# State space stage of a twelve-stage decoder: the causal convolution moved from VectorE to TensorE, the activations split off and done 1024 wide

## The chip, the core and the metric

One core of a Trainium2 chip runs the whole program. The time is the device time of one execution in microseconds, before as the median of three runs. In the profile PE is TensorE (PEld its weight loads), DVE is VectorE, ACT is ScalarE, POOL is GpSimd.

## What is computed

A decoder of four layers on 64 sequences of 64 tokens and 128 channels. The change lies in the seventh of its twelve stages, a Mamba-like state space block in float32:

```python
xr = x @ w_in + b_in                      # x normalised, 128 -> 512
xc, res = jnp.split(xr, 2, axis=-1)       # 256 channels each
u = jax.nn.silu(_causal_conv(xc, w_conv, b_conv))   # 4 taps along time
A = -jnp.exp(A_log)
dt, B, C = jnp.split(u @ w_x, [DTR, DTR + N], axis=-1)   # 64, 16, 16
delta = jax.nn.softplus(dt @ w_dt)
deltaA = jnp.exp(delta[..., None] * A)
deltaBu = delta[..., None] * B[:, :, None, :] * u[..., None]
h = a * h + bu                            # scan over the 64 steps, for each of N = 16 states
y = jnp.einsum('bldn,bln->bld', hs, C) + u * D
return y * jax.nn.silu(res) @ w_out
```

and `_causal_conv` is the bias plus the sum over k of `xp[:, k:k + l, :] * w_conv[k]`, with xp padded by three zero steps.

## The kernel before

The tokens are worked in NG = 8 groups g of 512 (eight sequences). Channels lie on the partitions, in two chunks c of 128, so a tile is 128x512. Within a group the 16 states k are the innermost loop. The program calls one (g, k) an iteration m = 16g + k; here it is called a slot.

Each engine has its own program, written out by hand, and semaphores join them. In slot m (line numbers are those of the profile):

- VectorE does `scan(m, 0)`, `contribute(m-1, 1)`, `scan(m, 1)`, `contribute(m, 0)` (L2131 the scan, L2139 its product with the row of C), then whatever is hung on this k: two convolution taps for the next group at k = 0 to 3 (`tap`, L2105 and L2108), `skipped` at the head of k = 1 (L2144), `residual` of the group before (L2149) and `ln.stats` at k = 4, `parts` (L2115 to L2122, splits B and C into three bf16 parts) at k = 6, `scale` (L658) at k = 9.
- ScalarE does `decay(m+1, 0)` (L2013, the exponential that the next scan reads), `copy_b(m+2)` (L2002), `decay(m+1, 1)`, then: `silus` at k = 4 (L1963, L1966), `copy_dt` at 5 (L1972), `high_part` at 6 (L1979), `step_size` at 7 and 8 (L1986, L1987), `softplus` at 9 (L1992 Exp, L1995 Ln), `copy_ln` and `channels` at 12 to 14 (L1947, L1955). Silu, Exp and Ln each want another table; ACT_TABLE_LOAD is put in where the function changes.
- TensorE does `accumulate(m-1, 0)` (L1898, hc times identity into a bank), `b_row(m+2)` and `c_row(m+1)` (L1876, which spread a row of B or C over the partitions), `accumulate(m-1, 1)`, then: `output` of the group before at k = 3 (L163), m2 and m3 at 4 (L1852), dt and bc at 5 and 6 (L1859), d0 and d1 at 7 and 8 (L1867), `turn` (L1845), m0, m1 at 12 to 14.
- GpSimd does the two products of `inputs(m+1)` (L2065), then `gated` at k = 2 (L2079), the norm's `rstd` at 5, `step_size` at 10 and 11 (L2070, L2073).

All the side steps of TensorE share one bank, `misc` (bank 7). `ssm_order` gives each its number; `take` waits until the step before it has been copied out (`misc_cp`), `have` waits until this one has been written (`misc_mm`). c_row is double buffered, b_row is not.

## Time and profile before

| | |
|---|---|
| median of 3 runs | 4207.73 us (4207.13 to 4212.16) |
| the profiled execution | 4205.07 us, its span 4203.3 us |
| busy shares | PE 88%, DVE 53%, ACT 37%, POOL 27% |
| the state space stage | from 2072.99 (first memset) to 2764.20 + 0.69 us (last residual) |
| granted TensorE clock, whole program | 0.912 |

Shares over the whole span say little here, since this change touches one stage of some 690 us; the stage's own windows and its timeline count.

### The profile page before, as it was taken

The numbers are of one execution on the slowest core, as the hardware profiler recorded it, in microseconds if no ns is written. First come the engines' busy times: TensorE is split into PE (matmuls) and PEld (weight loads), VectorE is DVE, ScalarE is ACT, GpSimd is POOL, SyncE is SP. The second block draws the span as 40 slices with busy tenths as digits, with TensorE's granted clock in tenths as the row PEclk, the third lists the DMA queues.
The fourth block names the chain that finished last, engine by engine and source line by source line (L and its number), as shares of the span: only waits on it lengthen the run. The fifth ranks groups of instructions, "written<-read, shape, count | busy, mean of one in ns | idle before, by whom it ended". The sixth has DMA issues, their size and how long they took to land. (4 is left out here: it accounts for less than half of the span.)

```text
span 4203.3 us, 78999 instructions
## 1 busy us (share of the span) xinstructions
PE 3692.2 (88%) x32473; PEld 2458.5 (58%) x32473; DVE 2212.7 (53%) x4913; ACT 1561.4 (37%) x2468; POOL 1145.7 (27%) x1165
## 2 busy tenths in 40 slices
PE   4988889998999988999867777786778999999998
PEld 2655567776777655666422222244448888767776
DVE  2645522222766655555478888855556556422222
ACT  3422233332111034222254555543225565434343
POOL 2534400001222154000056566643451011010111
PEclk8978889999999989999978878897789999999999
DMA  4000000000000010000100000000000000000000
GB/s 144 2 1 1 1 1 1 1 1 34 3 3 2 6 39 7 1 1 1 43 0 1 0 1 0 1 1 1 1 1 12 5 7 5 2 3 3 6 6 6
DMA packets 20276, 37.11 MB, mean 9 GB/s; under 512 B 848, under 2 KB 17488, under 8 KB 19280
## 3 DMA queue, kind: packets, MB, share of 16 engines
q1 hardware_dynamic: 19920, 32.07, 2.2%
q8 instruction: 260, 4.26, 0.4%
q14 instruction: 96, 0.79, 0.1%
HBM read 29.97 MB, written 2.10 MB: 8 GB/s over the span
## 5 line engine op out<-in xcount | busy, mean ns | idle before, releaser
L163 PEld LDWEIGHTS ps<-L_ffn_w,arena 128*128 128x128 f32 x5248 | 615.5, 193 | 58.3 <-issue 45.0
L649 POOL TENSOR_SCALAR arena<-arena 128x4 f32<-128x4 f32 x120 | 27.6, 230 | 2250.6 <-DVE arena L641 1913.7
L163 PE MATMUL ps<-L_ffn_w,arena 128*128 128x128 f32 x5248 | 627.1, 277 | 0.0
L751 PE MATMUL ps<-arena,L_ffn_w 128*128 128x512 f32 x1024 | 464.9, 597 | 0.0
L2065 POOL TENSOR_TENSOR arena<-arena 128x512 f32<-128x512 f32 x256 | 327.3, 1303 | 234.9 <-ACT arena L2002 234.3
L785 DVE SCALAR_TENSOR_TENSOR x_all<-ps,arena,x_all 128x128 f32<-128x128 f32 x512 | 144.2, 345 | 400.7 <-PE ps L163 400.7
L1898 PE MATMUL ps<-arena,const_w 128*128 128x512 f32 x512 | 325.1, 733 | 33.4 <-DVE arena L2144 20.7
L2131 DVE TENSOR_TENSOR_SCAN arena<-ps,arena 128x512 f32<-128x512 f32 x256 | 311.3, 1216 | 72.6 <-ACT ps L2013 56.1
L751 PEld LDWEIGHTS ps<-arena,L_ffn_w 128*128 128x128 f32 x1024 | 186.5, 192 | 186.7 <-issue 184.8
L163 PEld LDWEIGHTS ps<-L_attn_w,arena 128*128 128x128 f32 x1984 | 254.2, 197 | 61.5 <-issue 44.6
L163 PE MATMUL ps<-L_attn_w,arena 128*128 128x128 f32 x1984 | 283.7, 289 | 5.1 <-POOL arena L2079 2.7
L775 ACT ACTIVATE arena<-ps,L_ffn_w 128x512 f32<-128x512 f32 x256 | 174.5, 687 | 267.9 <-PE ps L751 267.8
L953 PE MATMUL ps<-arena,L_ffn_w 128*128 128x512 f32 x576 | 261.2, 596 | 0.8 <-ACT arena L986 0.8
L775 ACT ACTIVATE arena<-ps 128x512 f32<-128x512 f32 x256 | 152.1, 597 | 273.4 <-PE ps L751 273.2
L2013 ACT ACTIVATE ps<-arena,aneg 128x504 f32<-128x504 f32 x256 | 174.9, 683 | 200.9 <-DVE arena L2131 200.2
L785 DVE SCALAR_TENSOR_TENSOR arena<-ps,arena 128x128 f32<-128x128 f32 x256 | 72.1, 344 | 324.0 <-PE ps L163 324.0
L1876 PE MATMUL ps<-bcp,sel 96*128 96x512 bf16 x256 | 106.6, 451 | 112.3 <-DVE arena L2139 88.1
L1898 PEld LDWEIGHTS ps<-arena,const_w 128*128 128x128 f32 x512 | 108.5, 225 | 146.3 <-DVE arena L2139 77.8
L996 ACT ACTIVATE arena<-ps 128x512 f32<-128x512 f32 x144 | 86.0, 597 | 279.8 <-PE ps L953 231.7
L430 ACT ACTIVATE arena<-ps 128x1024 f32<-128x1024 f32 x96 | 98.4, 1025 | 235.1 <-PE ps L332 235.1
L1249 PE MATMUL ps<-arena,L_attn_w 128*128 128x512 f32 x384 | 183.8, 615 | 0.9 <-ACT arena L712 0.9
L1317 ACT ACTIVATE arena<-ps,L_attn_w 128x512 f32<-128x512 f32 x64 | 44.0, 687 | 347.5 <-PE ps L1249 347.5
(351 smaller groups left out, 6538.6 us busy)
## 6 DMA issues: line engine op xcount, KB each, us to landing
L_ffn_w<-L_ffn SPq DMA_DIRECT2D x1, 4312.0 KB, 14.1
L_ffn_w<-L_ffn SPq DMA_DIRECT2D x1, 4120.5 KB, 14.5
...
```

The costliest lines, as they stand in the source:

```text
L163: ins = pe.matmul(out, src[:, j * P:(j + 1) * P], w, start=(i == 0), stop=(bias is None and i == len(chunks) - 1))
L430: a.activation(pts(i), e.bank(0, 2), ACT.Copy).then_inc(s["pt_cp"], 1)
L751: pe.matmul(e.bank(f), up(x, f), xT(g), start=True, stop=True).then_inc(s["up_mm"], 1)
L775: a.activation(hidden(i)[:, f * GT:(f + 1) * GT], e.bank(f), func, bias=bias(x, f)).then_inc(s["act_done"], 1)
L785: ins = v.scalar_tensor_tensor(out=a, in0=e.bank(4 + i % 2)[:, j * D:(j + 1) * D], scalar=weight(j), in1=a, op0=ALU.mult, op1=ALU.add)
L953: pe.matmul(e.bank(2 * k + c), wt, src, start=True, stop=True).then_inc(s["gu_mm"], 1)
L1249: pe.matmul(e.bank(i), W(w)[:, col], xnT(g), start=True, stop=True).then_inc(s["qkg_mm"], 1)
L1876: return pe.matmul(out, e.sel[:, row:row + 1].broadcast_to([96, P]), bcp(g), start=True, stop=True)
L1898: pe.matmul(acc(c), e.ident, hc(m, c), start=(k == 0), stop=(k == N - 1)).then_inc(s["acc_mm"], 1)
L2013: a.activation(tiles(at(c), NB)[:, :, 1:S], tiles(delta(g, c), NB)[:, :, 1:S], ACT.Exp, scale=e.aneg[:, c * N + k:c * N + k + 1]).then_inc ...
L2065: q.tensor_tensor(bu(m, c), du(g, c), bs(m), ALU.mult).then_inc(s["bu_done"], 1)
L2131: v.tensor_tensor_scan(hs(m, c), at(c), bu(m, c), 0.0, ALU.mult, ALU.add).then_inc(s["hs_done"], 1)
```

## The change

The four taps become four matmuls that accumulate in the misc bank, each with a 128x128 diagonal matrix of tap weights as the stationary operand (`taps`, made once in the startup, in the free tiles pq and pk2) and a shifted view of xp as the moving one. ScalarE copies the result out with the bias (`raw`, Identity), also m2 and m3, and applies Silu later, in one place, to 1024 columns at a time; Exp and Ln of softplus, `step_size` and `gated` of GpSimd also become 1024 wide. `ssm_order` gets the steps cv0 and cv1, and the side steps move: output from k = 3 to 4, m2 and m3 to 5 and 6, silus from 4 to 6, dt and bc to 7 and 8, parts from 6 to 9, d0 and d1 to 10 and 11, softplus to 11, GpSimd's step_size to 12, ln.stats to 6, rstd to 7, scale to 11, turn, m0, m1 to 13 to 15.

```diff
--- before.py
+++ after.py
@@ -1791,9 +1791,11 @@
...
-    for step, g in [(x, 0) for x in "ln m0 m1 m2 m3 dt bc d0 d1".split()] + [(x, 1) for x in "ln m0 m1".split()]:
+    for step, g in [(x, 0) for x in "ln m0 m1 cv0 cv1 m2 m3 dt bc d0 d1".split()] + [(x, 1) for x in "ln m0 m1".split()]:
...
+        if g + 1 < NG:
+            use["cv0", g + 1], use["cv1", g + 1] = len(use), len(use) + 1
@@ -1810,20 +1812,21 @@
-        two = lambda t: lambda c: t[:, c * GT:(c + 1) * GT]
...
-        xp_all, tmp = room.take(2 * NB * (S + 3)), two(room.take(2 * GT))
+        xp_all, raw_u = room.take(2 * NB * (S + 3)), room.take(2 * GT)
+        taps = lambda c, i: (e.pq, e.pk2)[c][:, i * P:(i + 1) * P]
@@ -1850,6 +1853,18 @@
+            def convolve(c, g, which):
+                if which[0] == 0:
+                    take(("cv0", "cv1")[c], g)
+                    pe.wait_ge(s["misc_cp"], use[("m0", "m1")[c], g] + 1)
+                    if g == 0:
+                        pe.wait_ge(s["taps_done"], 1)
+                for i in which:
+                    ins = pe.matmul(tiles(misc, NB), taps(c, i), xp(c)[:, :, i:i + S],
+                                    start=(i == 0), stop=(i == 3))
+                if which[-1] == 3:
+                    ins.then_inc(s["misc_mm"], 1)
@@ -1898,8 +1913,12 @@
-            for step in ("m0", "m1", "m2", "m3"):
-                channels(step, 0)
+            channels("m0", 0)
+            channels("m1", 0)
+            for c in range(2):
+                convolve(c, 0, range(4))
+            channels("m2", 0)
+            channels("m3", 0)
@@ -1916,21 +1935,22 @@
-                if k == 3 and g >= 1:
+                if k == 4 and g >= 1:
...
                 if g + 1 < NG:
-                    if k == 4:
-                        channels("m2", g + 1)
-                        channels("m3", g + 1)
+                    if k < 4:
+                        convolve(k // 2, g + 1, ((0, 1), (2, 3))[k % 2])
                     if k in (5, 6):
-                        projected(("dt", "bc")[k - 5], g + 1)
+                        channels(("m2", "m3")[k - 5], g + 1)
                     if k in (7, 8):
-                        step_size(("d0", "d1")[k - 7], g + 1)
+                        projected(("dt", "bc")[k - 7], g + 1)
+                    if k in (10, 11):
+                        step_size(("d0", "d1")[k - 10], g + 1)
                 if g + 2 < NG:
-                    if k == 12:
+                    if k == 13:
...
-                    if k in (13, 14):
-                        channels(("m0", "m1")[k - 13], g + 2)
+                    if k in (14, 15):
+                        channels(("m0", "m1")[k - 14], g + 2)
@@ -1951,19 +1971,29 @@
...
-                    a.wait_ge(s["conv_done"], 2 * (g - 1) + c + 1)
+                    a.wait_ge(s["misc_mm"], use[("cv0", "cv1")[c], g - 1] + 1)
...
+            def raw(step, g):
+                c = int(step[-1]) % 2
+                have(step, g)
+                if step[0] == "c":
+                    if g >= 1:
+                        a.wait_ge(s["u_done"], 2 * g)
+                    out, bias = raw_u[:, c * GT:(c + 1) * GT], W("b_conv")[:, c:c + 1]
+                else:
+                    if g >= 2:
+                        a.wait_ge(s["yr_done"], 2 * (g - 1))
+                    out, bias = res(g, c), W("b_in")[:, 2 + c:3 + c]
+                a.activation(out, misc, ACT.Identity, bias=bias).then_inc(s["misc_cp"], 1)
             def silus(g):
-                for c in range(2):
-                    a.wait_ge(s["conv_done"], 2 * g + c + 1)
-                    if g >= 2 and c == 0:
-                        a.wait_ge(s["misc_mm"], use["y", g - 2] + 1)
-                    a.activation(u(g, c), tmp(c), ACT.Silu, bias=W("b_conv")[:, c:c + 1]).then_inc(s["u_done"], 1)
-                for c in range(2):
-                    have(("m2", "m3")[c], g)
-                    a.activation(res(g, c), misc, ACT.Silu, bias=W("b_in")[:, 2 + c:3 + c]).then_inc(s["misc_cp"], 1)
+                a.wait_ge(s["misc_cp"], use["m3", g] + 1)
+                if g >= 2:
+                    a.wait_ge(s["misc_mm"], use["y", g - 2] + 1)
+                a.activation(u_b(g), raw_u, ACT.Silu).then_inc(s["u_done"], 2)
+                a.activation(res_b(g), res_b(g), ACT.Silu).then_inc(s["res_done"], 1)
@@ -1988,11 +2018,9 @@
...
-                for c in range(2):
-                    a.activation(du(g, c), du(g, c), ACT.Exp, scale=-1.0).then_inc(s["sp_own"], 1)
-                a.wait_ge(s["sp_own"], 2 * (g + 1))
-                for c in range(2):
-                    a.activation(du(g, c), du(g, c), ACT.Ln, bias=1.0).then_inc(s["sp_done"], 1)
+                a.activation(du_b(g), du_b(g), ACT.Exp, scale=-1.0).then_inc(s["sp_own"], 1)
+                a.wait_ge(s["sp_own"], g + 1)
+                a.activation(du_b(g), du_b(g), ACT.Ln, bias=1.0).then_inc(s["sp_done"], 1)
@@ -2009,13 +2037,15 @@
                     if k == 0:
-                        a.wait_ge(s["dl_done"], 2 * g + c + 1)
+                        a.wait_ge(s["dl_done"], g + 1)
...
+            for step in ("cv0", "cv1", "m2", "m3"):
+                raw(step, 0)
@@ -2035,21 +2065,25 @@
                 if g + 1 < NG:
-                    if k == 4:
+                    if k in (1, 3):
+                        raw(("cv0", "cv1")[k // 2], g + 1)
+                    if k in (5, 6):
+                        raw(("m2", "m3")[k - 5], g + 1)
+                    if k == 6:
...
-                    if k == 5:
+                    if k == 7:
...
-                    if k == 6:
+                    if k == 8:
...
-                    if k in (7, 8):
-                        step_size(k - 7, g + 1)
-                    if k == 9:
+                    if k in (10, 11):
+                        step_size(k - 10, g + 1)
+                    if k == 11:
...
                 if g + 2 < NG:
-                    if k == 12:
+                    if k == 13:
...
-                    if k in (13, 14):
-                        channels(k - 13, g + 2)
+                    if k in (14, 15):
+                        channels(k - 14, g + 2)
@@ -2059,55 +2093,41 @@
                         if k == 0:
-                            q.wait_ge(s["du_done"], 2 * g + c + 1)
+                            q.wait_ge(s["du_done"], g + 1)
...
-            def step_size(c, g):
-                q.wait_ge(s["relu_done"], 2 * g + c + 1)
-                q.wait_ge(s["sp_done"], 2 * g + c + 1)
-                q.tensor_tensor(delta(g, c), delta(g, c), du(g, c), ALU.add).then_inc(s["dl_done"], 1)
-                q.wait_ge(s["dl_done"], 2 * g + c + 1)
-                q.wait_ge(s["u_done"], 2 * g + c + 1)
-                q.tensor_tensor(du(g, c), delta(g, c), u(g, c), ALU.mult).then_inc(s["du_done"], 1)
+            def step_size(g):
+                q.wait_ge(s["relu_done"], 2 * (g + 1))
+                q.wait_ge(s["sp_done"], g + 1)
+                q.tensor_tensor(delta_b(g), delta_b(g), du_b(g), ALU.add).then_inc(s["dl_done"], 1)
+                q.wait_ge(s["dl_done"], g + 1)
+                q.wait_ge(s["u_done"], 2 * (g + 1))
+                q.tensor_tensor(du_b(g), delta_b(g), u_b(g), ALU.mult).then_inc(s["du_done"], 1)
...
             def gated(g):
-                q.wait_ge(s["misc_cp"], use["m3", g] + 1)
-                for c in range(2):
-                    q.wait_ge(s["yo_done"], 2 * g + c + 1)
-                    q.tensor_tensor(u(g, c), u(g, c), res(g, c), ALU.mult).then_inc(s["yr_done"], 1)
+                q.wait_ge(s["res_done"], g + 1)
+                q.wait_ge(s["yo_done"], 2 * (g + 1))
+                q.tensor_tensor(u_b(g), u_b(g), res_b(g), ALU.mult).then_inc(s["yr_done"], 2)
...
-            step_size(0, 0)
-            step_size(1, 0)
+            step_size(0)
...
-                if k in (10, 11) and g + 1 < NG:
-                    step_size(k - 10, g + 1)
-                if k == 5 and g + 2 < NG:
+                if k == 12 and g + 1 < NG:
+                    step_size(g + 1)
+                if k == 7 and g + 2 < NG:
...
         @block.vector
         def _(v):
-            def tap(g, c, i):
-                t, w, x = tiles(tmp(c), NB), W("w_conv")[:, c * 4 + i:c * 4 + i + 1], xp(c)[:, :, i:i + S]
-                if i == 0:
-                    v.wait_ge(s["misc_cp"], use[("m0", "m1")[c], g] + 1)
-                    if g >= 1:
-                        v.wait_ge(s["u_done"], 2 * (g - 1) + c + 1)
-                    v.tensor_scalar(t, x, w, None, ALU.mult).then_inc(s["conv_own"], 1)
-                else:
-                    v.wait_ge(s["conv_own"], 3 * (2 * g + c) + i)
-                    v.scalar_tensor_tensor(out=t, in0=x, scalar=w, in1=t, op0=ALU.mult, op1=ALU.add
-                                           ).then_inc(s[("conv_own", "conv_done")[i == 3]], 1)
@@ -2161,7 +2181,8 @@
-                    tap(0, c, i)
+                    ins = v.tensor_scalar(taps(c, i), e.ident, W("w_conv")[:, 4 * c + i:4 * c + i + 1], None, ALU.mult)
+            ins.then_inc(s["taps_done"], 1)
@@ -2172,18 +2193,14 @@
-                if g + 1 < NG:
-                    if k < 4:
-                        for i in ((0, 1), (2, 3))[k % 2]:
-                            tap(g + 1, k // 2, i)
-                    if k == 6:
-                        parts(g + 1)
+                if k == 9 and g + 1 < NG:
+                    parts(g + 1)
...
                 if g + 2 < NG:
-                    if k == 4:
+                    if k == 6:
...
-                    if k == 9:
+                    if k == 11:
```

VectorE from k = 1 to k = 4 of a group, before. L2144 is skipped, L2149 residual, L635 and L641 ln.stats:

```order
L2144 SCALAR_TENSOR_TENSOR arena<-arena,L2_attn_w,ps 128x512 x2
L2131 SCALAR_TENSOR_TENSOR arena<-ps,arena 128x512
L2139 TENSOR_TENSOR arena<-arena,ps 128x512
...
L2108 SCALAR_TENSOR_TENSOR arena<-arena,L2_attn_w 128x512 x2
L2131 SCALAR_TENSOR_TENSOR arena<-ps,arena 128x512
...
L2149 TENSOR_TENSOR x_all<-ps,x_all 128x512
L635 BN_STATS arena<-x_all 128x6 x4
```

The same place with the change (L2164 skipped, L2151 scan, L2159 contribute, L2169 residual):

```order
L2164 SCALAR_TENSOR_TENSOR arena<-arena,L2_attn_w,ps 128x512 x2
L2151 SCALAR_TENSOR_TENSOR arena<-ps,arena 128x512
L2159 TENSOR_TENSOR arena<-arena,ps 128x512
...
L2169 TENSOR_TENSOR x_all<-ps,x_all 128x512
L2151 SCALAR_TENSOR_TENSOR arena<-ps,arena 128x512
```

The taps are gone from between the scans, ln.stats has left k = 4, and the residual is still the last of k = 4.

TensorE around the output of the group before (L163), before; a 128x512 x2 of L1876 is one slot's b and c row:

```order
L1876 MATMUL ps<-bcp,sel 128x512 x2
L1898 MATMUL ps<-arena,const_w 128x512
L163 MATMUL ps<-L2_attn_w,arena 128x128 x8
L1898 MATMUL ps<-arena,const_w 128x512
L1876 MATMUL ps<-bcp,sel 128x512 x2
L1898 MATMUL ps<-arena,const_w 128x512
L1852 MATMUL ps<-arena,L2_attn_w 128x512 x2
```

With the change (L1913 accumulate, L1891 rows, L1864 convolution, L1855 m2):

```order
L1864 MATMUL ps<-arena,pk2 128x512 x2
L1913 MATMUL ps<-arena,const_w 128x512
L1891 MATMUL ps<-bcp,sel 128x512 x2
L1913 MATMUL ps<-arena,const_w 128x512
L163 MATMUL ps<-L2_attn_w,arena 128x128 x8
L1913 MATMUL ps<-arena,const_w 128x512
L1891 MATMUL ps<-bcp,sel 128x512 x2
L1913 MATMUL ps<-arena,const_w 128x512
L1855 MATMUL ps<-arena,L2_attn_w 128x512
```

Two taps now stand at the end of each of the slots 0 to 3, the output at the end of slot 4, and m2 in slot 5. (A float32 matmul of this list is two MATMUL rows in the trace.)

ScalarE around the activations, before:

```order
L2013 ACTIVATE ps<-arena,aneg 128x8x63
L1963 ACT_TABLE_LOAD
L1963 ACTIVATE arena<-arena,L2_attn_w 128x512 x2
L1966 ACTIVATE arena<-ps,L2_attn_w 128x512 x2
L2013 ACT_TABLE_LOAD
L2013 ACTIVATE ps<-arena,aneg 128x8x63
```

With the change (L1989 raw, L1995 and L1996 the two Silus, L2041 decay):

```order
L1989 ACTIVATE arena<-ps,L2_attn_w 128x512
L1995 ACT_TABLE_LOAD
L1995 ACTIVATE arena<-arena 128x1024
L1996 ACTIVATE arena<-arena 128x1024
L2041 ACT_TABLE_LOAD
L2041 ACTIVATE ps<-arena,aneg 128x8x63
```

Between the two table loads nothing waits for TensorE any more; the last raw copy stands right ahead of them.

## Rows read from the trace of the kernel before

**Rows 1.** Groups by line and one line's own view (min/median/max ns), stage's window.

```profile
L2131 DVE TENSOR_TENSOR_SCAN arena<-ps,arena 128x512 f32<-128x512 f32 x256 | 311.3, 1216 | 72.6 <-ACT ps L2013 56.1 <-POOL arena L2065 14.5
...
L2108 DVE SCALAR_TENSOR_TENSOR arena<-arena,L_attn_w x48: 750/1631/1648, 2082.7 to 2639.5; 128x512 f32<-128x512 f32 x48
```

**Rows 2.** Windows: us, busy of PE, PEld, DVE, ACT, POOL, granted clock.

```profile
2356.00:2436.00 80.00, 58.17 (x125) 20.85 (x124) 66.71 (x88) 42.09 (x66) 45.52 (x37) 0.83 0.00 1
...
2676.00:2756.00 80.00, 60.49 (x146) 20.90 (x145) 76.90 (x92) 43.93 (x69) 59.34 (x48) 0.94 0.00 1
```

**Rows 3.** Timeline of VectorE, fourth group: start, us, then the instruction.

```profile
2364.50 1.22 DVE L2131 TENSOR_TENSOR_SCAN arena<-ps,arena 128x512 f32<-128x512 f32 x1
...
2370.17 1.39 DVE L2144 SCALAR_TENSOR_TENSOR arena<-arena,L_attn_w,ps 128x512 f32<-128x512 f32 x2
2371.49 1.21 DVE L2131 TENSOR_TENSOR_SCAN arena<-ps,arena 128x512 f32<-128x512 f32 x1
...
2389.03 1.21 DVE L2131 TENSOR_TENSOR_SCAN arena<-ps,arena 128x512 f32<-128x512 f32 x1
...
2392.45 0.68 DVE L2149 TENSOR_TENSOR x_all<-ps,x_all 128x512 f32<-128x512 f32 x1
```

**Rows 4.** The same timeline: VectorE's waits in one group (in brackets).

```profile
2400.77 1.22 DVE L2131 TENSOR_TENSOR_SCAN arena<-ps,arena 128x512 f32<-128x512 f32 x1 [3.05 <-ACT ps L2013]
...
2408.97 0.69 DVE L2115 TENSOR_TENSOR arena<-ps,bcp 32x512 f32<-32x512 f32 x1 [4.69 <-ACT bcp L1979]
...
2419.84 1.22 DVE L2131 TENSOR_TENSOR_SCAN arena<-ps,arena 128x512 f32<-128x512 f32 x1 [1.03 <-ACT ps L2013]
...
2425.46 1.22 DVE L2131 TENSOR_TENSOR_SCAN arena<-ps,arena 128x512 f32<-128x512 f32 x1 [0.84 <-ACT ps L2013]
...
2432.07 1.22 DVE L2131 TENSOR_TENSOR_SCAN arena<-ps,arena 128x512 f32<-128x512 f32 x1 [3.10 <-ACT ps L2013]
```

**Rows 5.** Waits over the stage: total us, times, longest.

```profile
DVE arena L2131 <- ACT ps L2013: 56.1, 29, 4.2
...
DVE arena L2115 <- ACT bcp L1979: 36.8, 8, 9.8
```

**Rows 6.** Timeline of ScalarE around silus.

```profile
2392.69 1.28 ACT L1963 ACT_TABLE_LOAD   x1
...
2400.05 0.68 ACT L2013 ACTIVATE ps<-arena,aneg 128x504 f32<-128x504 f32 x1
```

**Rows 7.** Groups by line, whole span: a 1024-wide activation from SBUF.

```profile
L424 ACT ACTIVATE arena<-arena 128x1024 f32<-128x1024 f32 x96 | 101.3, 1055 | 98.7 <-DVE arena L542 98.4
```

**Rows 8.** Timeline of TensorE: at either clock.

```profile
2387.11 2.60 PE L163 MATMUL ps<-L_attn_w,arena 128*128 128x128 f32 x16
...
2413.82 0.59 PE L1876 MATMUL ps<-bcp,sel 96*128 96x512 bf16 x1 [4.23 <-DVE arena L2139]
...
2424.62 0.60 PE L1876 MATMUL ps<-bcp,sel 96*128 96x512 bf16 x2
2425.05 1.88 PE L1898 MATMUL ps<-arena,const_w 128*128 128x512 f32 x4
...
2434.39 3.62 PE L1898 MATMUL ps<-arena,const_w 128*128 128x512 f32 x4
```

**Rows 9.** Timeline of GpSimd.

```profile
2385.61 2.95 POOL L2065 TENSOR_TENSOR arena<-arena 128x512 f32<-128x512 f32 x2 [2.99 <-ACT arena L2002]
...
2401.33 2.49 POOL L2065 TENSOR_TENSOR arena<-arena 128x512 f32<-128x512 f32 x2 [5.57 <-ACT arena L2002]
...
2429.66 1.26 POOL L2070 TENSOR_TENSOR arena<-arena 128x512 f32<-128x512 f32 x1 [1.14 <-ACT arena L1995]
```

**Rows 10.** Timeline of the startup.

```profile
2085.04 2.07 PE L1852 MATMUL ps<-arena,L_attn_w 128*128 128x512 f32 x2 [0.78 <-ACT arena L1955]
...
2092.10 3.31 PE L1859 MATMUL ps<-arena,L_attn_w 128*64 128x512 f32 x4 [0.78 <-ACT arena L1966]
...
2115.92 2.45 DVE L2131 TENSOR_TENSOR_SCAN arena<-ps,arena 128x512 f32<-128x512 f32 x2 [14.51 <-POOL arena L2065]
```

2 lines of the change are left out of this document (1 added, 1 removed).

## Prediction

> **What bounds the kernel now.** The change touches one stage, so the first view is the windows of the state space stage, not the shares of the page. In a middle window of 80 us VectorE is busy 66.7 us, TensorE 58.2, ScalarE 42.1, GpSimd 45.5; in the window that is mostly the last group, where no side work is left, VectorE is busy 76.9 of 80 [rows 2]. Then the timeline of VectorE, to see what fills a slot: two scans and two products. From 2389.03 to 2392.45 nothing else stands, so a bare slot is 3.42 us [rows 3]. Sixteen of them are 54.7 us. What a group takes above that is side work on VectorE and waits of VectorE. So the reader should look for (a) what else VectorE executes, and (b) which waits end last there. The waits of one group stand in [rows 4]; their totals over the stage are 56.1 us for decays that come late and 36.8 us for the high part of B and C, eight times, the longest of them (9.8) in the startup [rows 5]. A scan waiting for ScalarE does not mean that ScalarE is full; it is half idle. It means that one block of its program (table load, Silu, table load) is longer than the lead it has over the scans.
>
> **What the change removes.** *The taps.* From the scan at 2364.50 (k = 0) to the residual at 2392.45 (end of k = 4) are 27.95 us. Five bare slots are 17.1 and skipped is 1.32 (2371.49 less 2370.17), so the taps cost 9.5 us a group [rows 3]. Seven groups have them inside the loop: 66.5 us. In the first of these the scans of k = 1 wait for a decay that ScalarE issues late after its copies for group 1; the two taps of slot 0 lie under that wait and are worth nothing: less 2.2.
>
> That price contains contention: one tap with two operands takes from 0.75 to 1.65 us, its median 1.63 [rows 1], and the GpSimd pair beside taps takes 2.95 instead of 2.49 us [rows 9]. The GPSIMD Engine Reference of the Trainium skill (section 1, Specifications) says that GpSimd's SBUF interfaces are shared with VectorE and contend with VectorE instructions that have two SBUF inputs. That agrees with these rows. Priced without the contention, as VectorE work alone, eight taps at the minimum of 0.75 would be 6.0 us a group, 42 in all; priced by slots they are 66.5. I take the slots, since they hold what really stood on the path.
>
> *The wait of parts.* bc, high_part and parts were in one slot, so VectorE stood still for TensorE and ScalarE: 36.8 less the 9.8 of the startup is 27.0 us [rows 5]. With bc in slot 8 and parts in 9 there is a whole slot between: gain 27.0. The five instructions of parts stay.
>
> **What it moves.** *silus.* Before, ScalarE's block lasts from the table load at 2392.69 to the end of the next decay at 2400.73, 8.0 us, because m3 waits for the copy of m2 in its middle; the scan waits 3.05 [rows 4, 6]. Now two loads of 1.28 [rows 6], two Silus of 1.06 [rows 7] and the decay of 0.68, 5.4 us, behind the raw copy of m3. Counted from the start of slot 6: decay(7,1) ends at 3.7, TensorE has m3 at 3.9, raw ends 4.65, the decay for slot 8 ends at 10.0. VectorE wants it after two slots and ln.stats (1.2), at 8.05. Wait 2.0, in the last such group (no ln.stats) 3.2. Before, 3.05 in five groups, 3.65 in the first and 4.22 in the last of them (the longest of [rows 5]), 23 us; after, six by 2.0 and 3.2, 15. Gain 8.
>
> *d0, d1, softplus.* Before, in one group, 1.03 + 0.84 + 3.10 = 5.0 us [rows 4], over the seven about 32 (56.1 less the silus waits and the 0.9 after the start [rows 5]). Now softplus follows d1 in the same slot. From the relu of d1: two copies 1.1, Exp 1.06, load 1.28, Ln 1.06, load 1.28, decay 0.68, 6.5 us. When d1 is ready depends on TensorE's clock. Parts leave TensorE idle for some 3.7 us ahead of slot 10, and behind such an idle time of 4.23 us it ran at half clock, four matmuls in 3.62 us against 1.88 [rows 8]. At half clock d0 costs 1.1 us of wait in slot 10 and d1 4.5 in slot 11, together 5.6; at full clock 2.5. I take the half clock, by the nearest row: 39 in seven groups against 32, a loss of 7; the bound at full clock is a gain of 15.
>
> *GpSimd's step_size.* Two operations of 1024, each twice 1.26 [rows 9], now start together after Ln. Let X be the end of the first decay after softplus. Ln ended at X - 1.97, the sum at X + 0.6, the product at X + 3.2, and only then comes inputs(14, 0), done at X + 4.5. Its scan wants it at X + 3.4: a new wait of 1.1 us, 7.5 in all. inputs is what is queued behind it on GpSimd, and the scan waits for that.
>
> *The output of the group before.* It moved to k = 4 on TensorE, the residual on VectorE stays at k = 4. Before, a slot lay between, and the residual waited for nothing. Now TensorE starts the output after accumulate(m-1, 1), about 3.0 us into the slot plus what it lags, and needs 2.6 us [rows 8]; VectorE asks at 3.4. The lag comes from the convolution: a slot of 0 to 3 needs four accumulate matmuls and four for two taps (1.7 us each at full clock, from 1.88 less the drain) and two rows (0.43), 3.85 us against 3.42 [rows 8]. With skipped as slack it ends some 1.2 us behind at k = 4. So the residual waits 2.2 without lag, 3.6 with it. I take 3.6 for six groups and 2.2 for the last (no convolution in it): 23.8 lost.
>
> *Convolution on TensorE.* Its lead over VectorE absorbs the 0.4 us a slot: b_row may come over 2 us late before a scan waits. raw at k = 1 and 3 must wait for it, which delays a decay by up to 0.3; bc at slot 8 by up to 0.4. I charge 0.7 a group, 5 in all; bounds 0 and, at half clock, the rival below. The strided moving operand has no row; nearest is the contiguous one, 0.43 a matmul.
>
> *Startup and tail.* The tap diagonals (eight 128x128 products) lie under m0 and m1 and cost nothing. Then in line: m2 started at 2085.04, once m1 was copied [rows 10]; the first convolution starts there in its place; 5.2 us partly at half clock, raw 0.8, 3.5, raw 0.8, two round trips of 1.8 for m2 and m3, the first Silu 1.1: dt at 2100 instead of 2092.10 [rows 10]. With the wider first step of GpSimd 8.5 us lost. gated at the end waits for both halves: 0.8.
>
> **Sum.** 66.5 - 2.2 + 27 + 8 - 7 - 7.5 - 23.8 - 5 - 8.5 - 0.8 = 46.7. The profiled execution took 4205.07 us; 46.7 less is 4158.4. The median is 2.7 above the profiled one, so 4161.
>
> **Rivals.** *More gain.* TensorE, with less idle time, stays at full clock in slots 10 and 11 (22 more), and the output lags less (8 more), perhaps raw and bc cost nothing (5): 4126 to 4145. For it: 0.94 granted where slots are bare, against 0.83 [rows 2]. Against: the idle time behind parts stays.
>
> *Slower: TensorE becomes the bound in the convolution slots.* At half clock such a slot is 3.62 for accumulates, 3.62 for taps, 0.9 for rows, less drains 7.7 us, against 3.42 [rows 8]. Four slots are 17.1 us over, less a lead of 2.4: 14.7 by seven groups is 103, so 4264. It decides from a bit over two of the four slots at half clock, since 46.7 / 7 = 6.7 us. For it: the clock in the stage is 0.83 [rows 2], and the end of softplus now comes two slots later, nearer to k = 0. Against: once packed, TensorE came back to full clock within two to three slots, and in these slots it has almost no gap. On this the page TensorE: Matmul & The Clock Gate of the Trainium skill (section Why this matters for your kernels) says that sustained matmul work brings the full clock; by that rule too the slots would run full, and the time would be the forecast's.
>
> *Longer tail of softplus.* One or two more scans wait for GpSimd's late inputs, or the residual waits out a cold output (3.5 instead of 2.6): 2 to 4 us a group more, 4175 to 4193.
>
> *It does little.* Waits take the place of the taps: every slot from 0 to 3 ends with ScalarE held in raw, 5 to 7 us a group: 4196 to 4216.
>
> **Chances.** Forecast (4145 to 4175) 0.50, more gain 0.20, longer tail 0.14, little 0.07, slower 0.09. The range runs from 4128 to 4193 and leaves out the tail of more gain, little and slower. A measurement of this kernel tells about 0.2% (8.4 us) from no change. Faster by more than that (below 4199) 0.85, within it 0.06, slower 0.09.
>
> **What would show it.** In the profile after: no gap between scans in slots 0 to 3 but skipped, and a slot of 3.4 us there; parts without a wait; the first scan after the Silus waiting 2 us; the scan after softplus waiting 4 to 5 us, and the next one 1 us for GpSimd; the residual waiting 2 to 4 us for TensorE in seven groups, the longest new wait; the first scan near 2124. The period of a middle group comes to some 75 us (54.7 bare, 7 of side work, 13 of these waits). The prediction is wrong if slots 0 to 3 take over 4.5 us, if the convolution matmuls show half clock in most groups, or if the residual finds its output ready.

## The result and the profile after

Four runs of the changed kernel have a median of 4164.57 us (4160.2 to 4165.26), four of the kernel before beside them 4208.27. The ratio is 0.9892, its 95% interval 0.9875 to 0.9909, so 43.7 us less. The forecast was 4161 with a range from 4128 to 4193. The profiled execution of after is the slowest of its four, 4165.26 us, against 4205.07 before: 39.8 less, and against this number the parts are held below. Of the experiments' executions two, 5188.81 us in experiment 5 and 4912.06 us in experiment 9, ran at a granted clock of 0.67 and 0.71 instead of some 0.91, and every median below is that of the others.

VectorE's waits after, engine, line, releaser, then total us, times, longest. They answer to [rows 5] (L2151 is the scan, L2135 the start of parts, L2169 the residual):

```profile
DVE arena L2151 <- ACT ps L2041: 72.7, 26, 7.7
DVE arena L2135 <- ACT bcp L2009: 27.3, 1, 27.3
DVE x_all L2169 <- PE ps L163: 24.6, 8, 6.2
```

The wait for the high part stands eight times in [rows 5] and once here, in the startup. In its place the residual waits for TensorE eight times, and the scans wait longer for ScalarE. So the waits have not become less; they have moved: summed over the loop (defined below) those of VectorE are 83 us before and 91 after. The 24.6 of the residual hold 6.2 of the stage's tail.

The timeline of VectorE after, in the startup and in the second group (columns as in [rows 3]):

```profile
2105.81 0.69 DVE L2135 TENSOR_TENSOR arena<-ps,bcp 32x512 f32<-32x512 f32 x1 [27.33 <-ACT bcp L2009]
...
2124.15 2.44 DVE L2151 TENSOR_TENSOR_SCAN arena<-ps,arena 128x512 f32<-128x512 f32 x2 [15.58 <-POOL arena L2099]
...
2203.95 1.40 DVE L2164 SCALAR_TENSOR_TENSOR arena<-arena,L_attn_w,ps 128x512 f32<-128x512 f32 x2
...
2221.89 0.69 DVE L2169 TENSOR_TENSOR x_all<-ps,x_all 128x512 f32<-128x512 f32 x1 [2.84 <-PE ps L163]
...
2236.07 1.22 DVE L2151 TENSOR_TENSOR_SCAN arena<-ps,arena 128x512 f32<-128x512 f32 x1 [2.05 <-ACT ps L2041]
...
2243.77 0.86 DVE L2137 CAST bcp<-arena 32x512 bf16<-32x512 f32 x1
2244.66 1.37 DVE L2138 CAST bcm<-arena 32x512 bf16<-32x512 f32 x1
...
2264.88 1.22 DVE L2151 TENSOR_TENSOR_SCAN arena<-ps,arena 128x512 f32<-128x512 f32 x1 [6.07 <-ACT ps L2041]
...
2269.08 1.22 DVE L2151 TENSOR_TENSOR_SCAN arena<-ps,arena 128x512 f32<-128x512 f32 x1 [0.69 <-ACT ps L2041]
...
2279.36 1.40 DVE L2164 SCALAR_TENSOR_TENSOR arena<-arena,L_attn_w,ps 128x512 f32<-128x512 f32 x2
```

From one skipped to the next are 2279.36 less 2203.95, 75.4 us, where the prediction had some 75. The reader sees the four waits in their order: the output late for the residual (2.84), the Silu block (2.05), the block of softplus (6.07), GpSimd behind it (0.69). Parts have no wait any more, but two of their five instructions, the casts L2137 and L2138, are longer than before.

TensorE in the same group: first a slot of the convolution (L1864), then the idle time behind parts and d0, d1 (L1882).

```profile
2212.17 1.88 PE L1864 MATMUL ps<-arena,pk 128*128 128x512 f32 x4
...
2216.04 1.88 PE L1864 MATMUL ps<-arena,pk 128*128 128x512 f32 x4
...
2249.28 0.38 PE L1891 MATMUL ps<-bcp,sel 96*128 96x512 bf16 x1 [4.77 <-DVE arena L2159]
2249.50 1.83 PE L1913 MATMUL ps<-arena,const_w 128*128 128x512 f32 x2
2251.26 2.07 PE L1882 MATMUL ps<-arena,L_attn_w 64*128 64x512 f32 x2
...
2257.15 1.12 PE L1882 MATMUL ps<-arena,L_attn_w 64*128 64x512 f32 x2
```

One slot of the convolution takes 3.87 us (2216.04 less 2212.17) at full clock, and in the view no row between the two has a wait. The shifted views that the taps read cost nothing extra: four such matmuls (L1864) take 1.88 us, like four with a contiguous operand (L1913). Behind 4.77 us of idle time d0 takes 2.07 us, at the lower clock of 1.2 GHz (called half clock here); d1 takes 1.12, at 2.4 GHz again (full clock). d0 takes 2.07 in all seven groups, d1 in two of them, the ones where the wait of softplus is 7.70. ScalarE and GpSimd in the block of softplus:

```profile
2258.31 0.60 ACT L2016 ACTIVATE arena<-ps 128x512 f32<-128x512 f32 x1 [1.33 <-PE ps L1882]
...
2262.87 1.28 ACT L2041 ACT_TABLE_LOAD   x1
2264.16 0.68 ACT L2041 ACTIVATE ps<-arena,aneg 128x504 f32<-128x504 f32 x1
```

```profile
2262.99 2.34 POOL L2104 TENSOR_TENSOR arena<-arena 128x1024 f32<-128x1024 f32 x1 [4.02 <-ACT arena L2023]
2265.41 2.35 POOL L2107 TENSOR_TENSOR arena<-arena 128x1024 f32<-128x1024 f32 x1
2267.72 7.42 POOL L2099 TENSOR_TENSOR arena<-arena 128x512 f32<-128x512 f32 x6
```

The first product for the next slot starts at 2267.72 and ends some 1.23 us later, at 2268.95; the scan starts at 2269.08. The row of that scan names ScalarE, but the decay it reads had ended before; it waited for GpSimd. Experiment 2 tests this reading.

**Where the 39.8 went.** The profiles are cut at three points: the stage's first memset, the first scan, the last skipped, the last residual. From memset to first scan are 42.93 us before and 53.34 after, 10.4 lost. From the first scan to the last skipped (here called the loop) are 641.07 and 592.53, 48.5 gained. The rest of the stage is 7.21 and 7.79. Together 37.6; the other 2.2 lie ahead of the stage, which the change doesn't touch. The loop is the number that the experiments below are compared by, since it leaves out what differs ahead of the stage and behind it from one execution to the next.

### The profile page after: what moved, and what is told of

Same layout as the page of the kernel before. It is cut to its first block and busy times, and to the rows that moved or that the text cites. A ratio compares the mean times of both kernels' runs of the same rounds, so it can differ in the third digit from the quotient of the medians.

```text
span 4163.5 us, 79189 instructions
## 1 busy us (share of the span) xinstructions
PE 3689.2 (89%) x32601; PEld 2467.4 (59%) x32601; DVE 2152.8 (52%) x4857; ACT 1574.9 (38%) x2468; POOL 1131.4 (27%) x1141
## 5 line engine op out<-in xcount | busy, mean ns | idle before, releaser
L163 PEld LDWEIGHTS ps<-L_ffn_w,arena 128*128 128x128 f32 x5248 | 615.4, 193 | 58.3 <-issue 45.0
L163 PE MATMUL ps<-L_ffn_w,arena 128*128 128x128 f32 x5248 | 627.0, 277 | 0.0
L2151 DVE TENSOR_TENSOR_SCAN arena<-ps,arena 128x512 f32<-128x512 f32 x256 | 312.2, 1219 | 90.0 <-ACT ps L2041 72.7
L1913 PE MATMUL ps<-arena,const_w 128*128 128x512 f32 x512 | 290.5, 656 | 7.5 <-DVE arena L2159 6.4
L163 PE MATMUL ps<-L_attn_w,arena 128*128 128x128 f32 x1984 | 277.9, 285 | 5.8 <-POOL arena L2112 3.4
L163 PEld LDWEIGHTS ps<-L_attn_w,arena 128*128 128x128 f32 x1984 | 247.5, 193 | 59.5 <-issue 42.6
L2041 ACT ACTIVATE ps<-arena,aneg 128x504 f32<-128x504 f32 x256 | 174.6, 682 | 134.5 <-DVE arena L2151 134.3
L1891 PE MATMUL ps<-bcp,sel 96*128 96x512 bf16 x256 | 96.8, 412 | 114.6 <-DVE arena L2159 81.7
L2159 DVE TENSOR_TENSOR arena<-arena,ps 128x512 f32<-128x512 f32 x256 | 170.0, 664 | 0.0
## 6 DMA issues: line engine op xcount, KB each, us to landing
L_attn_w<-L_attn SPq DMA_DIRECT2D x1, 3153.0 KB, 21.2
```

What stands on the lines that cost most here:

```text
L163: ins = pe.matmul(out, src[:, j * P:(j + 1) * P], w, start=(i == 0), stop=(bias is None and i == len(chunks) - 1))
L1913: pe.matmul(acc(c), e.ident, hc(m, c), start=(k == 0), stop=(k == N - 1)).then_inc(s["acc_mm"], 1)
L2041: a.activation(tiles(at(c), NB)[:, :, 1:S], tiles(delta(g, c), NB)[:, :, 1:S], ACT.Exp, scale=e.aneg[:, c * N + k:c * N + k + 1]).then_inc ...
L2151: v.tensor_tensor_scan(hs(m, c), at(c), bu(m, c), 0.0, ALU.mult, ALU.add).then_inc(s["hs_done"], 1)
L2159: v.tensor_tensor(hc(m, c), hs(m, c), cbank(m), ALU.mult).then_inc(s["hc_done"], 1)
```

## The experiments

### 1. The residual into slot 5

The residual is put behind the second scan of slot 5, so that the output has time.

```diff
                 scan(m, 1)
+                if k == 5 and g >= 1:
+                    residual(g - 1)
                 contribute(m, 0)
...
-                if k == 4 and g >= 1:
-                    residual(g - 1)
```

> The changed kernel, with the residual of the group before moved on VectorE from the end of slot 4 into slot 5, behind its second scan; TensorE's output stays in slot 4. Theory (the residual waits 2.83 us in six groups and 1.5 in the last because output and residual share a slot): the wait goes, 18 us less than the changed kernel, about 4146; no wait at the residual. Rival (the wait only moves: m2 in slot 5 needs the bank that the residual frees, so raw, the decay behind it and a scan come late): less than 6 us gained, 4159 to 4165, and a new wait of a scan for ScalarE in slot 6 or 7.

Median 4161.14 us (4156.76 to 4161.58), ratio 0.9887 (0.9872 to 0.9902), loop 585.04: 7.5 us gained of 18.5 that had been waited. The theory had the wait gone, which it is, but 18 us less; the time is the rival's, though not by its mechanism alone. The wait of the residual is gone, and others are longer. The waits of VectorE over the run and the timeline of TensorE in the second group:

```profile
DVE arena L2151 <- ACT ps L2041: 83.5, 31, 7.7
```

```profile
2248.05 0.59 PE L1891 MATMUL ps<-bcp,sel 96*128 96x512 bf16 x1 [4.76 <-DVE arena L2159]
...
2250.27 2.07 PE L1882 MATMUL ps<-arena,L_attn_w 64*128 64x512 f32 x2
...
2256.84 2.07 PE L1882 MATMUL ps<-arena,L_attn_w 64*128 64x512 f32 x2
```

The scans wait 10.8 us more for ScalarE. Now d1 too is at half clock and the wait of softplus is 7.70 in six groups: 7.5 us more over the seven. The one after the Silus is 2.61 instead of 2.05, 3.4 us more. So a wait may be worth less than its length: part of what is freed comes back at the next block, here most of it where d1 is at half clock.

### 2. GpSimd's sum and product in two slots

The sum stays in slot 12, the product goes to 13, and `inputs` of one slot comes between.

```diff
                 if k == 12 and g + 1 < NG:
-                    step_size(g + 1)
+                    step_sum(g + 1)
+                if k == 13 and g + 1 < NG:
+                    step_product(g + 1)
```

> The changed kernel, with GpSimd's sum in slot 12 and its product in slot 13 instead of both in 12. Theory (the scan of slot 14 waits for inputs(14, 0) behind 4.7 us of step_size; the profile puts 0.69 us of it down to ScalarE's decay, which had long ended): the second wait after softplus, 0.69 us in seven groups, goes, about 5 us less, 4160. Rival (it is the decay, as the profile names it): nothing changes, 4164 to 4165, the wait stays.

Median 4157.54 (4155.6 to 4158.93), ratio 0.9882 (0.9865 to 0.9898), loop 586.62. GpSimd:

```profile
2259.45 2.34 POOL L2104 TENSOR_TENSOR arena<-arena 128x1024 f32<-128x1024 f32 x1 [4.70 <-ACT arena L2023]
2261.90 2.49 POOL L2099 TENSOR_TENSOR arena<-arena 128x512 f32<-128x512 f32 x2
2264.35 2.35 POOL L2109 TENSOR_TENSOR arena<-arena 128x1024 f32<-128x1024 f32 x1
```

The seven waits of 0.69 are gone, all of them, though every one was put down to ScalarE. So they were GpSimd's.

### 3. The whole of softplus one slot later

```diff
-                    if k == 11:
+                    if k == 12:
                         softplus(g + 1)
...
-                if k == 12 and g + 1 < NG:
+                if k == 13 and g + 1 < NG:
                     step_size(g + 1)
```

> The changed kernel, with softplus in slot 12 and GpSimd's step_size in 13, each one slot later; d1 stays in slot 11. Theory (d1 comes late at half clock and softplus starts only when d1 has been copied, so the two delays add up; in the kernel before they cost 0.84 and 3.10 in two slots): the wait after softplus falls from 6.07 to about 3.1, a wait of up to 1.1 stands in slot 12 or 13, together 1.5 to 2 us less in seven groups, 4150 to 4154. Rival (it is the length of the block alone, 6.5 us from the relu on): the wait stays over 5, 4160 to 4167.

Median 4156.7 (4144.21 to 4157.38), ratio 0.9872 (0.9857 to 0.9886), loop 584.87, 7.7 gained. The one wait becomes two, 1.87 after d1 and 2.91 after Ln in the second group, 4.8 instead of 6.07; the theory's 4150 to 4154 was missed by 3 us, and its rival, a wait still over 5, falls. Here the two causes are seen apart: 1.87 us are d1 that comes late from TensorE, 2.91 are Exp, Ln and two table loads. The total gets only a little shorter, because nothing of either cause has gone.

### 4. Filler matmuls in the idle time

Five float32 matmuls of 128x512 into the misc bank, whose result nobody reads, are put between the two rows of slot 10, right where TensorE stands idle for parts.

```diff
                 b_row(m + 2)
+                if k == 10 and g + 1 < NG:
+                    take("d0", g + 1)
+                    for _ in range(5):
+                        pe.matmul(misc, e.ident, xnT, start=True, stop=True)
                 c_row(m + 1)
```

> The changed kernel with five more float32 matmuls (identity times the transposed input, into the shared bank, where d0 overwrites them) on TensorE in slot 10 of seven groups, between the row of B and the row of C, where it stands idle 4.8 us. They are no part of the computation. Theory (the idle time beside parts drops the clock to half, and so d0, d1 and the accumulates around them come late): TensorE runs d0 and d1 at full clock, the wait after softplus falls from 6.07 to 2.5 to 3.5, some 18 to 25 us less, 4140 to 4147. Rival (the clock there does not matter, or the filler delays the row of C and takes back what it gives): within 5 us of the changed kernel, 4160 to 4169.

Median 4138.54 (4136.18 to 4142.66), ratio 0.9837 (0.9822 to 0.9851), loop 563.72: 28.8 us less than the changed kernel's, the largest step of any single edit to it, and a little more than the theory's 18 to 25. TensorE, then VectorE:

```profile
2240.33 4.46 PE L1939 MATMUL ps<-arena,const_w 128*128 128x512 f32 x10
2245.26 0.38 PE L1891 MATMUL ps<-bcp,sel 96*128 96x512 bf16 x1 [0.47 <-DVE arena L2163]
...
2246.43 1.12 PE L1882 MATMUL ps<-arena,L_attn_w 64*128 64x512 f32 x2
...
2249.85 1.12 PE L1882 MATMUL ps<-arena,L_attn_w 64*128 64x512 f32 x2
```

```profile
2250.17 2.76 DVE L658 TENSOR_SCALAR arena<-x_all,arena 128x128 f32<-128x128 f32 x4
...
2257.58 1.22 DVE L2155 TENSOR_TENSOR_SCAN arena<-ps,arena 128x512 f32<-128x512 f32 x1 [1.23 <-ACT ps L2045]
2261.80 1.22 DVE L2155 TENSOR_TENSOR_SCAN arena<-ps,arena 128x512 f32<-128x512 f32 x1 [0.70 <-ACT ps L2045]
```

The filler ends 0.47 us before the real work comes, so it delays nothing. d0 and d1 take 1.12 both, and the wait of softplus, 5.8 to 7.7 us in the changed kernel, is 1.24 in six groups and 3.91 in the last; over the seven, with the 1.03 that stood ahead of it in the last, 35.6 us less. The other waits are what they were (2.05, 2.83, 0.70). That only 28.8 of the 35.6 arrive has a reason that the rows show: `scale` (L658), which stands in slot 11 of six groups, now lies beside a pair of GpSimd (2249.84 to 2252.33) and takes up to 2.76 us for its four instructions instead of 1.11, in all 9.8 us more. The last group has no `scale`, and there the whole wait is seen. What the filler gives back is 28.8 / 7, some 4 us a group.

### 5. Before, with parts one slot later

In the kernel before, parts move to slot 7, d0 and d1 to 8 and 9, softplus to 10, `step_size` to 11 and 12. The taps stay on VectorE.

```diff
-                    if k in (7, 8):
-                        step_size(("d0", "d1")[k - 7], g + 1)
+                    if k in (8, 9):
+                        step_size(("d0", "d1")[k - 8], g + 1)
...
-                    if k == 6:
+                    if k == 7:
                         parts(g + 1)
```

> The kernel before (taps on VectorE) with one part of the change alone: parts one slot after bc and high_part (slot 7 instead of 6), and so d0 and d1 in 8 and 9, softplus in 10, GpSimd's step_size in 11 and 12. Theory (the wait of parts, 27 us over seven groups, was the price of sharing a slot, and can be had without the matmuls): 22 to 27 us less than before, 4181 to 4186, no wait at the first instruction of parts. Rival (TensorE and ScalarE are late by as much in the next slot, and a scan waits in its place): less than 8 us gained, over 4200.

Median 4199.96 us (4190.27 to 4201.86), ratio 0.9976 (0.9965 to 0.9988), 8 us less where 27 us of waits were in question; the theory had 22 to 27 less. The waits are read from one more execution of the same kernel:

> The same kernel as b1_parts_late, for an undisturbed profile: where the waits of parts went. By the theory left over from it, the wait at parts is gone, and scans wait in its place in the slots of bc, d0 and d1 or at softplus, at half clock; by its rival the wait at parts is still there. The time is that of b1_parts_late, about 4200.

The execution took 4199.72 us, its loop 631.87, 9.2 less than before. The waits, and the instructions of parts (busy us, mean ns):

```profile
DVE arena L2131 <- ACT ps L2013: 59.3, 30, 4.2
...
DVE arena L2115 <- ACT bcp L1979: 10.1, 1, 10.1
```

```profile
L2120 DVE TENSOR_TENSOR arena<-arena,bcm 32x512 f32<-32x512 f32 x7 | 9.5, 1364 | 0.2
L2118 DVE CAST bcm<-arena 32x512 bf16<-32x512 f32 x7 | 6.7, 961 | 0.2
L2122 DVE CAST bcp<-arena 32x512 bf16<-32x512 f32 x7 | 5.8, 825 | 0.2
```

Against 36.8 in [rows 5], 10.1 stay, all in the startup: 26.7 us of waits are gone. 3.2 come back as waits of the scans (59.3 against 56.1). The larger part, 13 us, comes back as longer instructions: in the kernel before, the same window of the loop has these means at 682, 415 and 418 ns, and L2117's at 417 against 663 here; the four differences are 1.88 us, seven times 13.2. A wait had kept parts away from GpSimd's work; without the wait they run beside it. So neither expectation had it: the wait is gone, as the theory says, scans wait in its place, as its rival says, but for 3.2 us only, and the larger part was in neither.

### 6. Before, with one tap of four

Only tap 0 is computed for each chunk, so three quarters of the convolution are left out.

```diff
-                        for i in ((0, 1), (2, 3))[k % 2]:
-                            tap(g + 1, k // 2, i)
+                        if k % 2 == 0:
+                            tap(g + 1, k // 2, 0)
```

> The kernel before, with three of the four taps left out (only tap 0 is applied, so the convolution is not computed); the schedule is that of before. It prices the taps. Theory (a tap costs what stands between the scans in the slots 0 to 3, with GpSimd beside it: 9.5 us a group for eight): six of eight go, 9.5 less two at 0.65 is 8.2 us in seven groups less 2 in the first, about 55 us, 4150 to 4157. Rival (only the work counts, 0.75 us a tap, the rest comes back as other waits): 6 x 0.75 in seven groups, 31 us, 4177.

Median 4144.92 (4140.9 to 4148.88), ratio 0.985 (0.9835 to 0.9864), loop 576.59, 64.5 less than before. That is nearly the whole price of the taps by slots (66.5), for the six two-operand taps of a group alone, and 5 us more than the fast end of the theory's range. Some 6 of it are waits: the one for the high part is 5.8 shorter (34.0 less 12.8 of the startup, 21.2 in the loop against 27.0), and what the other blocks wait less and more nearly cancels. The remaining 58 us are 1.4 for each of the 42 taps. So the price by slots was not too high, and the rival that the waits would swallow the taps falls.

### 7. Parts in the middle of slot 9

```diff
                 scan(m, 0)
+                if k == 9 and g + 1 < NG:
+                    parts(g + 1)
                 contribute(m - 1, 1)
                 scan(m, 1)
```

(The call at the end of the slot is taken out.)

> The changed kernel, with parts in slot 9 behind its first scan instead of at the slot's end. Theory (the two casts of parts take 0.86 and 1.37 us instead of 0.42 because the pair of inputs on GpSimd runs beside them; earlier in the slot GpSimd stands still): the casts take about 0.42 again, parts 2.9 us instead of 4.3, some 5 to 10 us less than the changed kernel, 4155 to 4160. Rival (the casts are slow for their place behind the difference, or TensorE's idle time grows by as much): the casts stay over 0.8, or the wait after softplus grows, 4160 to 4170.

Median 4146.42 (4145.2 to 4147.26), ratio 0.9853 (0.9837 to 0.9869), loop 573.94: 18.6 gained, more than the lengthened casts could give, and 9 us beyond the theory's range. The casts are at 416 and 415 ns again, but L2140 is at 1635 instead of 682, and the high part is waited for 1.03 us again. The gain is elsewhere:

```profile
2248.01 0.59 PE L1891 MATMUL ps<-bcp,sel 96*128 96x512 bf16 x1 [4.07 <-DVE arena L2159]
2248.39 3.36 PE L1913 MATMUL ps<-arena,const_w 128*128 128x512 f32 x4
...
2252.97 1.12 PE L1882 MATMUL ps<-arena,L_attn_w 64*128 64x512 f32 x2
```

TensorE's idle time now ends with four accumulates that have piled up. They take the half clock (3.36 us), and d0 behind them is at full clock. In all seven groups d0 and d1 take 1.12 us, and the wait of softplus is 4.13 to 4.77 in four of them and 1.21 to 1.22 in three, instead of 5.8 to 7.7. Of the 3 us between the two kinds most is no gain: in the three `scale` (L658) takes 2.91 to 3.14 us beside GpSimd instead of 1.12, as in experiment 4, and the scans come later by that. About 1 us is real (groups of 73.0 and 74.1 us, from residual to residual): in the four, the full clock comes back later and d0 with it. The full clock at d0 and d1 goes with the gain, as in experiment 4, but here it was not changed alone.

### 8. The changed kernel with half of the convolution matmuls

Two of the four tap matmuls of each chunk are left out, so half of the convolution isn't computed.

```diff
-                for i in which:
+                for i in which[-1:]:
                     ins = pe.matmul(tiles(misc, NB), taps(c, i), xp(c)[:, :, i:i + S],
-                                    start=(i == 0), stop=(i == 3))
+                                    start=True, stop=True)
```

> The changed kernel, with two of the four tap matmuls left out for each chunk (taps 0 and 2, so the convolution is not computed). It prices the convolution on TensorE. Theory (at full clock TensorE lags the scans by 0.4 us a slot and no scan waits for that; only the residual sees the lag): the wait of the residual falls from 2.83 to about 1.5, nothing else moves, 5 to 10 us less, 4155 to 4160. Rival (TensorE bounds the slots 0 to 3): over 20 us less, below 4145.

Median 4157.07 (4151.39 to 4159.72), ratio 0.9877 (0.9862 to 0.9892), loop 583.08. The residual waits 1.49 in each group instead of 2.83: TensorE's lag from the convolution was 1.3 us at the output, and the 1.49 that stay come from output and residual being in one slot. The waits of 0.40, 1.08 and 0.80 in the first group are gone as well. The loop is 9.4 us shorter, which is about all that the convolution costs in TensorE's slots: with one tap in each (3.87 less 0.86, some 3.0 us by estimate) they are shorter than the scans' 3.42 and leave no lag. The rival falls.

### 9. The changed schedule with the taps on VectorE

All moves of the change are kept; the four taps are VectorE instructions in slots 0 to 3 again, and `cv0`, `cv1` and their raw copies are gone.

```diff
-                    if k < 4:
-                        convolve(k // 2, g + 1, ((0, 1), (2, 3))[k % 2])
...
                 contribute(m, 0)
+                if k < 4 and g + 1 < NG:
+                    for i in ((0, 1), (2, 3))[k % 2]:
+                        tap(g + 1, k // 2, i)
```

> The changed kernel with the convolution taken back to VectorE alone (eight taps in the slots 0 to 3, writing the same tile, bias in the first tap); everything else, the later slots, the Silus and softplus 1024 wide, GpSimd's wide steps, stays as changed. Theory (the gain is the taps; what the new schedule gives at parts and silus it gives back at the residual, softplus and GpSimd): within 12 us of the kernel before, 4196 to 4212. Rival (the schedule is worth some 25 us by itself, as the sum's 27 for parts says): 4175 to 4190.

Median 4224.28 us (4221.57 to 4232.01), ratio 1.0047 (1.0026 to 1.0067), loop 661.48. So the moves alone make the kernel 18 us slower than before by the medians (4206.59 beside it) and 20.4 by the loop, and the convolution on TensorE is worth 69.0 us of loop (661.48 less 592.53). Neither the theory nor its rival had this kernel that slow, and the recorded sum does not have it either. Taken without the taps (66.5 less 2.2) it leaves -17.6 us, but in this are the lag behind the convolution (8.4), raw and bc (5) and the startup (8.5), which this kernel hasn't got (its startup takes 42.93 us, as before). Without them the sum has the moves at 4 us faster than before. The profile shows where the difference lies, in us of the loop, gained (+) or lost (-) against the kernel before: the wait of parts +27.0, silus +5.6, softplus -16.0, GpSimd -4.8, the residual -21.2, the casts of parts -9.8, the first group -0.6, together -19.8 of the -20.4. One part of it is the output:

```profile
2235.85 0.58 PE L1877 MATMUL ps<-bcp,sel 96*128 96x512 bf16 x1 [2.96 <-DVE arena L2152]
...
2237.93 3.59 PE L163 MATMUL ps<-L_attn_w,arena 128*128 128x128 f32 x16
...
2411.41 1.95 PE L163 MATMUL ps<-L_attn_w,arena 128*128 128x128 f32 x16
```

Without the convolution TensorE has gaps of 1.7 to 3.3 us between the taps, and in four of seven groups it writes the output at half clock: 3.59 us against 1.95, and there the residual waits 4.15 to 4.18 us instead of 1.49. In the windows of the loop the granted clock is 0.83 before, 0.82 here, and 0.91 with the convolution on TensorE.

### 10. Filler, split GpSimd step and late residual together

Experiments 1, 2 and 4 in one kernel; the diff is theirs.

> The changed kernel with three of the edits together: the filler matmuls in slot 10, GpSimd's product in slot 13, the residual in slot 5. Theory (three waits of different places; the 1.6 us a group that the residual's edit lost again was the clock at d1, which the filler now holds): 26 for the filler, 5 for GpSimd, 14 to 18 for the residual, together about 4117 to 4122. Rival (they share a cover, and the gains don't add): over 4130.

Median 4116.52 us (4110.96 to 4121.47), ratio 0.9793 (0.977 to 0.9816), loop 544.13. This is the fastest version, 90 us less than the kernel before beside it (4206.59) and 48 less than the changed one. VectorE's waits in the second group, all of them:

```profile
2209.33 1.22 DVE L2160 TENSOR_TENSOR_SCAN arena<-ps,arena 128x512 f32<-128x512 f32 x1 [0.19 <-ACT ps L2045]
2224.07 1.22 DVE L2160 TENSOR_TENSOR_SCAN arena<-ps,arena 128x512 f32<-128x512 f32 x1 [2.62 <-ACT ps L2045]
2249.61 1.22 DVE L2160 TENSOR_TENSOR_SCAN arena<-ps,arena 128x512 f32<-128x512 f32 x1 [1.23 <-ACT ps L2045]
```

4.0 us of waits where the changed kernel has 11.7. The loops of the single edits would add up to 28.8 + 5.9 + 7.5 = 42.2 us; it is 48.4, for d0 and d1 are at full clock in all seven groups, and the 7.5 us that the late residual gave back there in experiment 1 stay. The granted clock in the loop is 0.97.

### 11. The same with parts in the middle of slot 9

> As c2_three, and parts behind the first scan of slot 9. Theory (parts at its place 1.4 us quicker, 1.0 us of wait for high_part in front): 0 to 6 us less than c2_three. Rival (the filler finds its idle time elsewhere, and d0 comes late): slower than c2_three by up to 10.

Median 4159.1 (4150.72 to 4161.84), ratio 0.9887 (0.9865 to 0.9909), loop 586.46, 42 us slower than experiment 10 for one more edit that had gained 18.6 by itself. TensorE:

```profile
2246.26 0.59 PE L1891 MATMUL ps<-bcp,sel 96*128 96x512 bf16 x1 [4.07 <-DVE arena L2168]
2246.65 3.62 PE L1913 MATMUL ps<-arena,const_w 128*128 128x512 f32 x4
...
2250.49 5.02 PE L1939 MATMUL ps<-arena,const_w 128*128 128x512 f32 x10
```

The idle time now lies ahead of slot 10's first row, and the filler stands behind it. The accumulates take the half clock, then the filler takes 5.02 us on the path, and the row of C comes late: scans wait 1.84 and 4.77 behind it. The mechanism is the rival's, the size far beyond its 10 us. A filler helps only where the idle time is.

## Why the prediction was right, and which terms were off

The time was 3.6 us above the forecast, and the steps that it named are the ones that the trace shows. That it came so close is in part luck: in the loop the casts and softplus are 17.6 us worse than forecast, GpSimd, the residual and the first group 10.7 better. The terms of the loop, in us, gained (+) or lost (-); measured are busy times and waits of the two profiles, and the row of the taps is what is left of the loop beside the others, so the sum closes by construction:

| term | predicted | measured |
|---|---|---|
| taps | +66.5 | +66.3 |
| parts: the wait | +27.0 | +27.0 |
| parts: the instructions | 0 | -9.8 |
| silus | +8 | +7.6 |
| d0, d1, softplus | -7 | -14.8 |
| GpSimd's `step_size` | -7.5 | -4.8 |
| residual behind the output | -23.8 | -18.5 |
| first group, raw and bc | -7.2 | -4.5 |
| sum of the loop | +56.0 | +48.5 |
| startup | -8.5 | -10.4 |
| tail | -0.8 | -0.6 |

**Taps.** Right, by slots and not by the minimum of 0.75, as far as a remainder can show it; what holds it up are experiments 6 and 9. What is left of the loop once the waits and the casts are taken off is 56.5 us less; with the casts' 9.8 this is 66.3. Experiment 9 gives 69.0 with the waits that change with the convolution, experiment 6 gives 58 in instructions for three taps of four. Priced as VectorE's work alone, 42, the forecast would have been 24 us too high. The contention of [rows 1, 9] is real time of the path.

**The wait of parts.** It is gone as forecast, but "The five instructions of parts stay" is the step that failed. They are as many as before, but not as long. Means in the loop after (busy us, mean ns):

```profile
L2138 DVE CAST bcm<-arena 32x512 bf16<-32x512 f32 x7 | 9.6, 1368 | 0.2
L2137 DVE CAST bcp<-arena 32x512 bf16<-32x512 f32 x7 | 6.0, 857 | 0.2
```

In the kernel before they are 415 and 417 ns: 1.39 us more, seven times 9.8. Before, VectorE's wait let GpSimd finish its pair of products; now parts start as soon as the slot's last product is done (2243.04), when GpSimd is just beginning its next pair (2243.08, 2.67 us). In the startup, where GpSimd does nothing, they still take 0.42 and 0.41. The GPSIMD Engine Reference of the Trainium skill (section 1, Specifications) says that GpSimd shares its SBUF interfaces with VectorE and contends with VectorE instructions in a mode that uses two ports or with two SBUF inputs. The prediction cites it for the taps alone. The rows agree with it for the subtraction in parts, which has two SBUF inputs (L2120 in experiment 5, L2140 in 7: 0.68 us, beside GpSimd up to 1.64), and for L2135, which has one input in PSUM and is 689 ns everywhere. The casts have one input; that they fall under the rule would need them to be in the mode with two ports, which no row here shows. The length goes with GpSimd's work and not with the instruction: in experiment 7 the casts start while GpSimd stands still and take 0.42, and the subtraction, which starts beside its product, takes 1.64.

**Silus.** 2.05 to 2.07 in six groups and 3.22 in the last; predicted 2.0 and 3.2.

**d0, d1, softplus.** The mechanism was right (the half clock behind parts, experiment 4), the size was not. I had 5.6 us a group; measured are 5.80 to 7.70 in one wait. Part of it may be that parts, with the longer casts, left TensorE idle for 4.77 us where I had put 3.7; and in two groups d1 too is at half clock (7.70). The price itself stands on two rows: the 3.62 us for four matmuls in [rows 8] are not those behind the idle time of 4.23 (they stand 20 us later, behind 2.54 and 0.85), but right behind the 4.23 two accumulates take 1.91 and d0 2.07, the same clock. The bound for the full clock, 2.5 us a group, was a little low: with the filler the wait is 1.24, but 1.6 more lie in the longer `scale`, together 2.9.

**GpSimd.** One operation of 1024 takes 2.34 us, not twice 1.26, so the scan waits 0.69 instead of 1.1.

**Residual.** 2.83 instead of 3.6, in the last group 1.49 instead of 2.2. The output takes 1.95 us at full clock with TensorE packed; the 2.60 of [rows 8] lies between that and the 3.59 at half clock of experiment 9. The lag of the convolution is 1.34 (experiment 8); the prediction writes 1.2 for it and reckons with 1.4 (3.6 less 2.2).

**Raw and bc.** Nothing in the middle groups; in the first, 5.4 us in four waits (3.09, 0.40, 1.08, 0.80), less the 0.9 that stood there before.

**Startup.** 10.4 in the profiled run, of which 3.0 belong to that execution: bc and d0 were at half clock there and dt in part (bc 3.62 us), where in experiment 1, with the very same startup, bc takes 1.90 and the first scan comes 50.30 us behind the memset. 7.4 is what the change costs there, against 8.5. With it the profiled gain would be 42.8, close to the 43.7 of the medians.

**The rivals.** TensorE was not the bound in slots 0 to 3: they ran at full clock in 3.87 us, absorbed by the lead. The rival of more gain was right that the clock decides, and wrong that the change would bring it by itself: experiment 4 with a filler reaches 4138.5, within its range. The longer tail of softplus came in its size (7.70 in two of seven groups) and not by its causes: no further scan waited for GpSimd, and the output was at full clock in the loop; it was d1 at half clock. The change that does little was excluded by the slots without gaps.

**The signs.** The slots without gaps, parts without a wait, the 2 us behind the Silus and the residual in six groups came as written. The wait behind softplus was 5.8 to 7.7 and not 4 to 5. The first scan at 2124.15, forecast near 2124, is luck: the stage began 2.2 us earlier and its startup took 1.9 more. The period, 75.4 against 75, is in part luck too: the waits in it are 11.7 instead of 13, the side work 9 instead of 7.

Two things stay open. Why d1 is at half clock in two of seven groups and not in the others, with the same work ahead of it, was not settled. And the losses in experiment 9 are read from its profile; no run undoes the moves one by one.
